# A hand-ordered attention and adapter kernel: one pool of seven PSUM banks, and an order planned by a clock of the engines

## The chip, the core and the metric

The kernel runs on one core of a Trainium2 chip. The core has five engines with queues of their own, each working strictly through its own list: TensorE (PE, with its weight loads shown as PEld), VectorE (DVE), ScalarE (ACT), GpSimd (POOL) and SyncE (SP), which here only issues DMA transfers. PE can write only into PSUM, which has eight banks of 512 float32 per partition; DVE and ACT read the banks and so set them free. The metric is the device time of one execution in microseconds.

## What is computed

One transformer block on 4 sequences of 1024 tokens with 256 channels: layer norm with modulation, attention with 16 heads of 16 channels, then a second layer norm and a mixture of adapters in which each group of tokens takes one of 8 experts by its reconstruction loss. Cut to what matters here:

```python
h = _layernorm(x) * (1 + ca) + sa
qkv = h @ qkv_w.T                                    # per head: q, k, v of 16 channels
scores = einsum('bhqd,bhkd->bhqk', q, k) * scale
probs = softmax(scores, axis=-1)
out = einsum('bhqk,bhkd->bhqd', probs, v)
x = x + ga * (out @ proj_w.T + proj_b)
h = _layernorm(x) * (1 + cb) + sb
base = h @ W_base + b_base
hid = relu(h @ W_enc[n] + b_enc[n])                  # 8 experts
losses = mean((hid @ W_dec[n] + b_dec[n] - h) ** 2)
top1 = argmin(losses)                                # one expert for a group of tokens
mid = relu(h @ W_down[top1] + b_down[top1])
x = x + gb * (base + mid @ W_up[top1] + b_up[top1])
```

## The kernel before, in words

The work of PE falls into three kinds, and the text calls them by these names.

**Scores.** For each of 4 sequences, 4 groups of 4 heads and 2 halves of the queries there is one "hq" (32 in all, in the order of the table `SEQ`). An hq has 32 tiles `M` (queries on the partitions, 512 keys in the free dimension; DVE reduces each to a row maximum, line 1293) and 8 units of 4 tiles `E` (keys on the partitions, 512 queries; ACT takes the exponential of each into `P`, line 1118). That makes 1024 M tiles and 1024 E tiles. Each is one matmul whose contraction is 48 or 50 rows, on the upper or the lower 64 partitions, so that two neighbours of unlike halves run side by side. The maxima of an hq go through `mmax` (DVE, POOL), a short transpose `mturn` (PE), a copy (ACT, `mT`) and four small DMAs into two rows of `QO`, and only then can the E tiles of that hq be computed. The M tiles therefore run ahead of the E tiles, by `LEAD` = 48 tiles here.

**P V.** For each of the 256 units, 4 products of `P` with `V` (17 columns each, side by side) accumulate into the bank `pO`. After 8 units ACT copies it to `osb`, from where it goes through DRAM (`oput`, `oget`, `orec`, `osum`, `onorm`) to the attention output `AT`.

**Side products.** All the rest: `ln1turn` (transposes), `qk` and `v` (projections), `proj`, `xturn`, `enc` (hidden layers of all experts), `gsq` and `half` (the losses), `base`, `select`, `mid`, `out`. Each has an eviction on DVE or ACT. The `qk` results are split into `hi` and `lo` and moved by 12 DMAs per group into `QO` and `KO` (`copy`). The evicting ACT step waits for the copies of the group before, since it overwrites `hi`.

**What sets the order.** `order()` writes one list of steps; every engine goes through the same list and takes from it what is its own. `plan()` names the unit from which a side step may come, and `before()` the steps that it needs, each with a lag in units. The main loop then repeats a fixed cycle: a burst of `BURST` = 3 E tiles and 3 M tiles (M and E in turn), then either one or two units of P V or some side products, whose number follows from a credit (`SHARE`) for each sequence. A side product comes in at most two pieces (`PIECES`).

**Banks.** `pO` has one bank for itself. The other seven are three for M (`MB`), three for E (`EB`) and one for side products (`XB`); a side product also takes a bank of M or E when its own is in use, and score tiles never take the one of the side products. `Steps` writes down which bank a step has. Before a tile PE waits until the reader of the bank's last contents is done (`free0` to `free6`).

The last sequence has a tail written out by hand (`first`, `base`, `now`, `fill`), after the last P V.

## Time and profile before

| | us |
|---|---|
| median of 3 runs | 1006.09 |
| lowest and highest | 1005.58, 1010.55 |
| span of the profiled execution | 1004.2 |
| PE busy | 962.7 (96%) |
| DVE busy | 813.2 (81%) |
| ACT busy | 661.7 (66%) |
| POOL busy | 284.4 (28%) |
| first P V unit to last P V unit | 69.8 to 958.2 |

The profile is read in this way. Busy shares tell which engine is short of time, but a PE that waits inside a burst of pipelined matmuls still looks nearly busy, since the ends of matmuls are modelled. So the starts of matmuls in the timeline are read, from the start of one group of equal work to the start of the next. The waits of PE show in the idle time of its weight loads (PEld) with the instruction that ended it. `x` counts are instructions; a matmul on plain float32 operands (`V` with `P`, `wqkv_s`, `wpg`, `wug`) is recorded as two instructions. `SPq`, `ACTq` are DMA issues on the queues of these engines.

### The profile page before, as it was taken

The numbers are of one execution on the slowest core, as the hardware profiler recorded it, in microseconds if no ns is written. First come the engines' busy times: TensorE is split into PE (matmuls) and PEld (weight loads), VectorE is DVE, ScalarE is ACT, GpSimd is POOL, SyncE is SP. The second block draws the span as 40 slices with busy tenths as digits, with TensorE's granted clock in tenths as the row PEclk, the third lists the DMA queues.
The fourth block names the chain that finished last, engine by engine and source line by source line (L and its number), as shares of the span: only waits on it lengthen the run. The fifth ranks groups of instructions, "written<-read, shape, count | busy, mean of one in ns | idle before, by whom it ended". The sixth has DMA issues, their size and how long they took to land.

```text
span 1004.2 us, 16485 instructions
## 1 busy us (share of the span) xinstructions
PE 962.7 (96%) x5794; PEld 480.8 (48%) x5794; DVE 813.2 (81%) x1657; ACT 661.7 (66%) x1295; POOL 284.4 (28%) x391
## 2 busy tenths in 40 slices
PE   6989999999899999999999999999999999999998
PEld 5444344343344445554454454545454455644476
DVE  4789989899688887788888888788778788889455
ACT  2148787887577777667668786766657767666831
POOL 4210133022155241200336431300237413116320
PEclk9879999999899999999999999999999999999999
DMA  6850051242550513242223511404424311132001
GB/s 180 141 92 23 12 107 45 56 95 71 80 96 12 96 34 66 44 85 81 70 87 60 85 44 45 75 13 78 130 70 80 58 29 35 38 96 77 29 6 48
DMA packets 47890, 66.93 MB, mean 67 GB/s; under 512 B 12139, under 2 KB 32112, under 8 KB 47796
## 3 DMA queue, kind: packets, MB, share of 16 engines
q1 hardware_dynamic: 46572, 65.00, 29.9%
q0 software_dynamic: 384, 0.79, 0.5%
q8 instruction: 46, 0.75, 0.3%
q14 instruction: 36, 0.29, 0.1%
q10 hardware_dynamic: 852, 0.09, 0.1%
HBM read 27.48 MB, written 12.59 MB: 40 GB/s over the span
## 4 chain that ended last, share of the span: by engine, by line
PE 77%; DVE 9%; ACT 5%; issue 2%; POOL 2%; DMA 2%; SPq 1%; ACTq 0%; DVEq 0%; POOLq 0%
PE pE L811 25%; PE pO L811 22%; PE pX L811 18%; PE pM L811 11%; DVE mx L1293 4%; ACT P L1118 2%; DMA QO<-lo 1%; ACT h1T L1159 1%; DVE h2f L1454 1%; ACT h2f L1205 1%; ACT hi L1175 1%; DVE lo L1374 1%; SPq L1867 0%; DVE junk L1430 0%; DMA P<-in_wmod 0%
## 5 line engine op out<-in xcount | busy, mean ns | idle before, releaser
L1293 DVE TENSOR_REDUCE mx<-pM 128x1 f32<-128x512 f32 x1006 | 629.7, 682 | 76.7 <-PE pM L811 71.4
L1118 ACT ACTIVATE P<-pE 128x512 f32<-128x512 f32 x996 | 526.7, 601 | 181.1 <-PE pE L811 177.8
L811 PE MATMUL pM<-KO,QO 48*128 48x512 f32 x1006 | 370.7, 455 | 6.8 <-DMA QO<-lo 3.3
L811 PE MATMUL pE<-QO,KO 50*128 50x512 f32 x996 | 349.2, 438 | 11.9 <-ACT h1T L1159 5.1
L811 PEld LDWEIGHTS pE<-QO,KO 50*128 50x128 f32 x996 | 164.9, 187 | 234.1 <-issue 125.1
L811 PE MATMUL pO<-P,V 128*17 128x512 f32 x2048 | 257.9, 598 | 5.1 <-ACT P L1118 5.1
L811 PEld LDWEIGHTS pM<-KO,QO 48*128 48x128 f32 x1006 | 164.3, 187 | 41.3 <-DVE mx L1293 28.8
L811 PEld LDWEIGHTS pO<-P,V 128*17 128x17 f32 x2048 | 40.5, 96 | 103.2 <-issue 88.1
L1695 POOL CAST mh<-mxc 128x16 fp32r<-128x16 f32 x32 | 6.5, 203 | 285.7 <-DVE mxc L1302 285.5
L811 PE MATMUL pX<-h1T,wqkv_s 128*128 128x512 f32 x112 | 59.2, 642 | 1.9 <-DVE lo L1374 1.5
L1754 POOL TENSOR_TENSOR Hs<-h2f,Hs 128x512 fp32r<-128x512 f32 x28 | 35.7, 1284 | 83.6 <-ACT Hs L1235 68.3
L1374 DVE SCALAR_TENSOR_TENSOR lo<-pX,cst,hi 128x512 fp32r<-128x512 f32 x27 | 20.2, 750 | 28.9 <-ACT hi L1175 28.8
L1175 ACT ACTIVATE hi<-pX,cst 128x512 fp32r<-128x512 f32 x27 | 18.6, 690 | 25.7 <-PE pX L811 20.8
L1721 POOL TENSOR_TENSOR AT<-AT,asum 128x512 f32<-128x512 f32 (+1 forms) x16 | 20.7, 1295 | 48.1 <-DMA asum<-wsum 48.1
L1748 POOL TENSOR_TENSOR Xs<-Xr,Xs 128x512 fp32r<-128x512 f32 x16 | 20.5, 1283 | 38.4 <-ACT Xs L1225 37.4
L811 PEld LDWEIGHTS pX<-h1T,wqkv_s 128*128 128x128 f32 x112 | 18.9, 193 | 23.2 <-issue 19.0
L1792 POOL TENSOR_SCALAR Xr<-x,mv,rs 128x256 f32<-128x256 f32 x24 | 29.3, 1227 | 0.9 <-POOL rs L1780 0.2
L1659 POOL TENSOR_SCALAR xin<-xin,mv,rs 128x256 f32<-128x256 f32 x24 | 29.3, 1228 | 0.5
L811 PE MATMUL pX<-Xs,Hs 128*128 128x258 f32 x192 | 28.6, 294 | 0.2 <-ACT h1T L1159 0.2
L811 PEld LDWEIGHTS pX<-Xs,Hs 128*128 128x128 f32 x192 | 24.4, 189 | 7.6 <-issue 6.2
L1125 ACT ACTIVATE osb<-pO 128x512 f32<-128x512 f32 x32 | 19.3, 602 | 11.1 <-PE pO L811 10.8
L811 PE MATMUL pX<-wqkv_s,h1T 128*128 128x256 f32 x88 | 23.8, 400 | 0.0
(301 smaller groups left out, 1023.4 us busy)
## 6 DMA issues: line engine op xcount, KB each, us to landing
outs<-osb SPq DMA_DIRECT2D x31, 256.0 KB, 2.9
KO<-hi SPq DMA_DIRECT2D x56, 128.0 KB, 4.0
QO<-hi SPq DMA_DIRECT2D x56, 128.0 KB, 5.1
x<-in_x SPq DMA_DIRECT2D x20, 256.0 KB, 3.6
out<-x SPq DMA_DIRECT2D x16, 256.0 KB, 2.1
AT<-outs SPq DMA_DIRECT2D x15, 256.0 KB
asum<-wsum SPq DMA_DIRECT2D x15, 256.0 KB
KO<-lo SPq DMA_DIRECT2D x28, 128.0 KB, 3.6
```

The lines of the kernel that those rows point to most:

```text
L811: return e.matmul(o, lhsT, rhs, start=start, stop=stop)
L1118: e.activation(P[:, u % 3, j, :], bank(s), ACT.Exp).then_inc(*empties(s))
L1125: e.activation(osb[:, :], pO[:, :], ACT.Copy).then_inc(s_osb, 1)
L1159: a = e.activation(h1T[:, c, 256 * k:256 * k + 256], bank(s)[:, 256 * c:256 * c + 256], ACT.Identity, bias=modT[:, c, b:b + 1], scale=modT ...
L1175: e.activation(halves(gi)[0][:, cs], bank(s), ACT.Identity, scale=qscale).then_inc(s_hi, 1)
L1293: e.tensor_reduce(mx[:, hq % 2, k:k + 1, kh], bank(s), AX.X, ALU.max, negate=True).then_inc(*empties(s))
L1374: e.scalar_tensor_tensor(out=lo_[:, cs], in0=bank(s), scalar=qscale, in1=hi_[:, cs].bitcast(F), op0=ALU.mult, op1=ALU.subtract).then_inc(* ...
L1659: a = e.tensor_scalar(xt[:, t, :], xt[:, t, :], mv1[:, k, t, 0:1], rs1[:, k, 1, t:t + 1], ALU.subtract, ALU.mult)
L1721: e.tensor_tensor(rows, rows, asum[0:p1, :], ALU.mult).then_inc(s_at, 1)
L1748: e.tensor_tensor(Xs[:, t0:t0 + 2, 1, 0:D], Xr[:, t0:t0 + 2, :], Xs[:, t0:t0 + 2, 0, 0:D].bitcast(F), ALU.subtract).then_inc(s_Xl, 1)
L1754: e.tensor_tensor(Hs[:, t % 4, :, 1, :], h2f[:, t % 2, :].rearrange("p (a n) -> p a n", a=4), Hs[:, t % 4, :, 0, :].bitcast(F), ALU.subtra ...
L1792: a = e.tensor_scalar(Xr[:, t % 4, :], x2[:, t, :], mv2[:, t, 0:1], rs2[:, 1, t:t + 1], ALU.subtract, ALU.mult)
```

## The change

The seven banks become one tensor `pS` that every kind of step shares. `order()` no longer follows a fixed cycle; it keeps a clock for the two halves of PE (`lane`), for ACT, DVE, POOL and SP (`engine`) and for each bank (`free`), with a table of durations (`WORK`, `GROUP`, `TILE`, `UNIT`, `ENTER`), and asks at each point what comes next:

- in a burst of scores it goes on as long as a bank is free by that clock, and takes M or E by which evicting engine has less work waiting (`BIAS` favours M; M may lead E by up to `AHEAD` = 64 tiles);
- otherwise it takes P V units that are ready, or one *group* of a side product, or goes back to scores. A side product now has up to six groups (`GROUPS`), and scores or P V may stand between them, while its bank stays taken;
- background steps (`quiet`) and copies come by the clock, not by units, and `before()` has no lags.

In `SEQ` the third and fourth group of heads are taken half by half, and in `plan()` the side steps after attention are due in two halves, the first 15 units earlier; `prep` is due at unit 20 for all sequences. Two operands are widened: `wdh`, `wdl` become parts of one tensor, and `mid` runs with 128 columns of weights of which 64 count; `wug` and `mid` have 128 rows, the added ones zero. DVE gets two more memsets at the start and POOL one. The number of score tiles, P V units and side matmuls is the same. The code also has a way to run a side group on one half of the array (`h` not None, `s_over`); the planner never asks for it. The tail written by hand has the same products in the same order.

Cut to its core (comments on steps that are the same are left out):

```diff
-BURST = 3
-SHARE = (1.2, 1.8, 1.8, 2.4)
-LIGHT = 66
-MB, EB, XB = (0, 1, 2), (3, 4, 5), 6
+BANKS = 7
+GROUPS = {"qk": 2, "v": 4, "proj": 4, "enc": 6, "half": 4, "gsq": 4, "base": 4, "mid": 6, "out": 6,
+          "ln1turn": 1, "xturn": 1}
-SEQ = [(gi, c) for gi in range(4 * NB - 3) for c in range(2)]
-SEQ += [(4 * NB - 3 + g, c) for c in range(2) for g in range(3)]
+SEQ = [(4 * b + g, c) for b in range(NB - 1) for g, c in (
+    (0, 0), (0, 1), (1, 0), (1, 1), (2, 0), (3, 0), (2, 1), (3, 1))]
+SEQ += [(4 * NB - 4 + g, c) for g, c in (
+    (0, 0), (0, 1), (1, 0), (2, 0), (3, 0), (1, 1), (2, 1), (3, 1))]
+TILE, UNIT, AHEAD = 228, 853, 64
+SOON, PATIENCE = 200, 2000
+BIAS, ONE, FED, TICK = 300, 900, 500, 700
+LATE, NEED = 0, 5
+LIGHTLY, HEAVY = (500, 500, 500, 0), (4000, 4000, 3000, 2000)
+ENTER = {"S": 260, "V": 110, "X": 110}
...
-            halves = ((B - 23, (0, 1)), (B, (2, 3))) if q == LAST else ((B, (0, 1, 2, 3)),)
+            halves = ((B - (23 if q == LAST else 15), (0, 1)), (B, (2, 3)))
...
-            u = B + (20 if b == LAST else 53)
+            u = B + 20
...
     if kind == "qk":
-        return [(("ln1turn", b, 2 * a[1] + i), 1) for i in range(2)] + [(("moved", 4 * b + a[0] - 1), 2)]
+        return [("ln1turn", b, 2 * a[1] + i) for i in range(2)] + [("moved", 4 * b + a[0] - 1)] + (
+            [("v", b, k) for k in range(4)] if a == (3, 1) else [])
...
+    def score(r):
+        t = flow.lane[r]
+        if flow.bank(t + LATE) is None:
+            return None
...
+        return min(found, key=lambda f: flow.backlog(f[0]) - BIAS * (f[0] == "DVE"))[1]
...
+    while min(e) < 2 * NU:
+        background()
+        t = flow.now()
+        found = [score(0), score(1)]
+        s = found[0] or found[1]
+        if mode == "S" and s:
+            if all(found) and sorted(flow.free)[1] <= max(flow.lane) + LATE:
+                flow.lane = [max(flow.lane)] * 2
+                r = 0 if found[0][0] == "M" else 1
+                take(found[r], r)
+                take(score(1 - r) or found[1 - r], 1 - r)
+                continue
+            if not all(found):
+                take(s, found.index(s))
+                continue
+        n = weighable()
+        busy = min(flow.backlog("ACT"), flow.backlog("DVE"))
...
+        if mode != "S" and p > (HEAVY if busy < FED else LIGHTLY)[min(pv // UB, LAST)] and side():
+            continue
+        if mode != "S" and s and (busy < FED or vacant(t + ENTER["S"] + 300) >= NEED):
+            enter("S")
+            continue
+        if n >= 2 or n and (min(e) >= 2 * (pv + 3) or mode == "V" or busy > ONE):
+            weigh(min(n, 2))
+            continue
+        if (p > LIGHTLY[min(pv // UB, LAST)] or not s) and side():
+            continue
...
-        pM = ctx.enter_context(nc.psum_tensor("pM", [128, 3, 512], F))
-        pE = ctx.enter_context(nc.psum_tensor("pE", [128, 3, 512], F))
+        pS = ctx.enter_context(nc.psum_tensor("pS", [128, BANKS, 512], F))
         pO = ctx.enter_context(nc.psum_tensor("pO", [128, 512], F))
-        pX = ctx.enter_context(nc.psum_tensor("pX", [128, 512], F))
...
+            if kind == "mid":
+                c, i = divmod(g, 3)
+                sl = slice(512 * s[2], 512 * s[2] + 512)
+                wh, wl = (wdhl[r, k:k + 2, :].rearrange("p a n -> p (a n)") for k in (c, 2 + c))
+                return thrice(o, wh, wl, h2h[r, c, sl], h2l[r, c, sl])[i:i + 1]
```

What this makes of PE's list, counted over the whole of it (a group is a row of equal kind; the transposes `mturn` count as side products):

| | scores: groups | P V: groups | side: groups | matmuls |
|---|---|---|---|---|
| before | 342 (314 of 6 tiles, 22 of 4, 5 of 12, 1 of 16) | 189 (67 of two units) | 192 | 2048, 1024, 1407 |
| after | 405 (48 of 2 tiles, 163 of 4, 148 of 6, 34 of 8, 12 longer) | 239 (17 of two units) | 247 | 2048, 1024, 1407 |

Of these, 81, 63 and 26 groups stood between the first and the 64th P V unit, and now 87, 61 and 37; from there to the 240th unit 232, 116 and 142, and now 289, 165 and 187.

The first place is PE early in the first sequence, where there is hardly any side work. `free3` and the like are the banks that a tile waits for. Before:

```order
L811 MATMUL pE<-QO,KO 128x512 [waits free5]
L811 MATMUL pM<-KO,QO 128x512 [waits free0]
L811 MATMUL pE<-QO,KO 128x512 [waits free3]
L811 MATMUL pM<-KO,QO 128x512 [waits free1]
L811 MATMUL pE<-QO,KO 128x512 [waits free4]
L811 MATMUL pM<-KO,QO 128x512 [waits free2]
L811 MATMUL pO<-P,V 17x512 x4
```

and now:

```order
L1072 MATMUL pS<-KO,QO 128x512 [waits free3]
L1072 MATMUL pS<-QO,KO 128x512 [waits free0]
L1072 MATMUL pS<-KO,QO 128x512 [waits free2]
L1072 MATMUL pS<-QO,KO 128x512 [waits free5]
L1072 MATMUL pS<-KO,QO 128x512 [waits free4]
L1072 MATMUL pS<-QO,KO 128x512 [waits free1]
L1072 MATMUL pS<-QO,KO 128x512 [waits free6]
L1072 MATMUL pS<-KO,QO 128x512 [waits free0]
L1072 MATMUL pO<-P,V 17x512 x4
```

The burst went from six tiles on banks tied to their kind to eight tiles on any bank; the eighth takes the bank of the second.

The second place is PE at the side work of the third sequence (beside the scores of the fourth), at its last transposes and at loss products. `cst,Xr` are the transposes `xturn`, `Hs` are products of `gsq`, `Xs,Hs` of `half`. Before:

```order
L971 MATMUL pX<-cst,Xr 128x128 [waits X,free6]
L971 MATMUL pX<-cst,Xr 128x128 x3
L971 MATMUL pE<-cst,Xr 128x128 [waits free3]
L971 MATMUL pE<-cst,Xr 128x128 x3
L811 MATMUL pE<-QO,KO 128x512 [waits free4]
L811 MATMUL pM<-KO,QO 128x512 [waits free0]
L811 MATMUL pE<-QO,KO 128x512 [waits free5]
L811 MATMUL pM<-KO,QO 128x512 [waits free1]
L811 MATMUL pE<-QO,KO 128x512 [waits free3]
L811 MATMUL pM<-KO,QO 128x512 [waits free2]
L811 MATMUL pX<-Hs 128x256 [waits Hl,free6]
```

and now, at the same transposes:

```order
L1243 MATMUL pS<-cst,Xr 128x128 [waits X,free2]
L1243 MATMUL pS<-cst,Xr 128x128 x3
L1072 MATMUL pS<-KO,QO 128x512 [waits free4]
L1072 MATMUL pS<-KO,QO 128x512 [waits free5]
L1072 MATMUL pS<-QO,KO 128x512 [waits d_m13,free1]
L1072 MATMUL pS<-QO,KO 128x512 [waits d_m10,free3]
L1072 MATMUL pS<-KO,QO 128x512 [waits free0]
L1072 MATMUL pS<-QO,KO 128x512 [waits free6]
L1072 MATMUL pO<-P,V 17x512 x4
L1243 MATMUL pS<-cst,Xr 128x128 [waits free2]
L1243 MATMUL pS<-cst,Xr 128x128 x3
L1072 MATMUL pS<-KO,QO 128x512 [waits free4]
```

The second transpose, which took the bank of an E tile (`free3`) just ahead of a burst whose last pair wanted it back, now stands behind that burst and a P V unit and takes the bank of the first transpose.

The third place is PE at the `enc` products of the same side work. Where one `enc` (six matmuls) stood in one piece, it is now cut by score groups:

```order
L1072 MATMUL pO<-P,V 17x512 x4
L1072 MATMUL pS<-weh,h2h 128x512
L1072 MATMUL pS<-KO,QO 128x512 [waits free4]
L1072 MATMUL pS<-QO,KO 128x512 [waits d_m02,free3]
L1072 MATMUL pS<-KO,QO 128x512 [waits free2]
L1072 MATMUL pS<-QO,KO 128x512 [waits free0]
L1072 MATMUL pS<-KO,QO 128x512 [waits free1]
L1072 MATMUL pS<-QO,KO 128x512 [waits free5]
L1072 MATMUL pS<-wel,h2h 128x512
L1072 MATMUL pS<-weh,h2l 128x512
L1072 MATMUL pS<-weh,h2h 128x512 [waits free3]
L1072 MATMUL pS<-QO,KO 128x512 [waits free4]
```

One matmul of an `enc` stands alone between a P V unit and a burst, and the product keeps its bank over the burst.

## Rows read from the trace of the kernel before

**Rows 1.** The page: busy time of the engines, and TensorE's clock in 40 slices.
```profile
PE 962.7 (96%) x5794; PEld 480.8 (48%) x5794; DVE 813.2 (81%) x1657; ACT 661.7 (66%) x1295; POOL 284.4 (28%) x391
...
PEclk9879999999899999999999999999999999999999
```

**Rows 2.** Busy time by stretch: us, PE, PEld, DVE, ACT, POOL (x), PEclk, DMA share, GB/s.
```profile
69.80:257.20 187.40, 184.37 (x1108) 75.53 (x1110) 169.79 (x298) 148.49 (x289) 38.48 (x61) 0.99 0.29 63
257.20:918.50 661.30, 642.05 (x3967) 320.53 (x3966) 544.10 (x1103) 455.09 (x896) 198.67 (x256) 0.99 0.30 65
...
958.20:1004.20 46.00, 40.80 (x277) 35.72 (x276) 29.32 (x103) 9.24 (x18) 7.03 (x9) 1.00 0.08 27
```

**Rows 3.** Timeline of PE, 793 to 806 us: start, length, instruction, count, idle before.
```profile
793.05 1.91 PE L811 MATMUL pO<-P,V 128*17 128x512 f32 x16
794.89 0.50 PE L811 MATMUL pE<-QO,KO 50*128 50x512 f32 x1
...
795.23 0.63 PE L811 MATMUL pE<-QO,KO 50*128 50x512 f32 x2
...
795.80 0.50 PE L811 MATMUL pX<-weh,h2h 128*128 128x512 f32 x1
...
797.52 0.39 PE L811 MATMUL pE<-wel,h2h 128*128 128x512 f32 x1
797.75 0.40 PE L811 MATMUL pE<-weh,h2l 128*128 128x512 f32 x1
798.08 0.50 PE L811 MATMUL pE<-QO,KO 50*128 50x512 f32 x1
...
799.42 1.05 PE L811 MATMUL pO<-P,V 128*17 128x512 f32 x8
800.41 0.50 PE L811 MATMUL pE<-QO,KO 50*128 50x512 f32 x1
...
803.35 0.49 PE L811 MATMUL pE<-QO,KO 50*128 50x512 f32 x1
...
805.08 0.50 PE L811 MATMUL pE<-QO,KO 50*128 50x512 f32 x1 [0.99 <-ACT h2f L1205]
...
805.51 0.74 PE L811 MATMUL pX<-Hs 128*128 128x256 f32 x4
```

**Rows 4.** Timeline of PE: the first and the last groups of scores and of P V.
```profile
26.84 1.19 PE L811 MATMUL pM<-KO,QO 48*128 48x512 f32 x3 [3.33 <-DMA QO<-lo]
...
69.77 1.91 PE L811 MATMUL pO<-P,V 128*17 128x512 f32 x8
...
954.44 0.50 PE L811 MATMUL pM<-QO,KO 50*128 50x512 f32 x1
...
955.11 1.05 PE L811 MATMUL pO<-P,V 128*17 128x512 f32 x8
957.15 1.05 PE L811 MATMUL pO<-P,V 128*17 128x512 f32 x8 [0.99 <-ACT P L1118]
```

**Rows 5.** Waits, whole span: us in total, times, longest us.
```profile
PEld pE L811 <- ACT P L1118: 60.4, 88, 0.9
PEld pM L811 <- DVE mx L1293: 29.7, 92, 2.2
```

**Rows 6.** The page: costliest groups of the two evicting engines.
```profile
L1293 DVE TENSOR_REDUCE mx<-pM 128x1 f32<-128x512 f32 x1006 | 629.7, 682 | 76.7 <-PE pM L811 71.4
L1118 ACT ACTIVATE P<-pE 128x512 f32<-128x512 f32 x996 | 526.7, 601 | 181.1 <-PE pE L811 177.8
```

**Rows 7.** Timeline, 264 to 267 us, and the clock's stretch behind it.
```profile
264.85 0.69 ACT L1175 ACTIVATE hi<-pX,cst 128x512 fp32r<-128x512 f32 x1 [4.60 <-DMA QO<-lo]
...
266.07 1.05 PE L811 MATMUL pO<-P,V 128*17 128x512 f32 x8 [3.17 <-ACT P L1118]
...
268.00:274.00 6.00, 6.00 (x13) 2.35 (x12) 2.66 (x6) 2.54 (x6) 0.58 (x3) 0.50 0.08 30
```

**Rows 8.** Groups by shape: a matmul of `mid`, on 64 columns of weights.
```profile
L811 PE MATMUL pX<-h2h,wdl 128*64 128x512 f32 x12 | 4.7, 394 | 0.0
```

More of the change, by code:

```diff
@@ new lines, in order @@
+    late |= {("out", q, i) for i in range(4)} | {("xsq", q, 1)} | set(sums(q, 0)) | set(sums(q, 1))
+    rest = [s for k in ("quiet", "short", "long") for s in waiting[k] if s not in late]
+    while rest:
+        s = min(rest, key=lambda s: max([done.get(p, 1e18) for p in before(s)] + [flow.now()]))
+        rest.remove(s)
+        if s[0] in BANKED:
+            flow.alone(s, sum(GROUP.get(s[0], 300) for g in range(groups(s))) if s[0] in GROUPS else 300)
+            out[-1:] = whole(s)
+            del flow.banks[s]
+        else:
+            flow.quiet(s)
@@ L1019, in tensor @@
+                    if part.over:
+                        a.then_inc(s_over, 1)
+                    elif part.last:
                         a.then_inc(*fills(s))
@@ L1468, in vector @@
                     dve.wait_ge(*emptied(*s))
-                elif kind == "gsq":
+                elif kind == "gsq" and last:
                     b, i, th = s[1:]
```

915 lines of the change are left out of this document (511 added, 404 removed).

## Prediction

> **What bounds the kernel now.** I read the page first. PE is busy for 96% of the span, DVE for 81%, ACT for 66%, and the clock was at its upper level nearly throughout [rows 1]. So PE is the engine to look at, with DVE behind it. The busy time by stretch says where: up to the 64th P V unit DVE is busy for 169.8 of 187.4 us (91%), from there to the 240th unit for 544.1 of 661.3 us (82%), ACT for 79% and 69% [rows 2].
>
> A PE at 96% can still be waiting, so next comes the timeline of PE, read from the start of one group of equal work to the start of the next. A clean burst of six score tiles takes 0.91 us, from 794.89 to 795.80, and two P V units take 1.84 us, from 793.05 to 794.89; one unit takes 0.99 us, from 799.42 to 800.41 [rows 3]. The next clean thing to read is the pitch inside a group. The second pair of tiles starts 0.34 us after the first [rows 3], and further pairs follow at 0.23 us, as do matmuls of the same 512 columns (797.52 to 797.75). The last matmul of a group is followed by a start of another kind only after 0.33 us (797.75 to 798.08) [rows 3]. So one change of kind costs some 0.1 us. In sum I price a group of scores at 0.228 us a pair plus 0.205 us (0.89 for six tiles), P V at 0.858 a unit plus 0.125 us, and each further group of side work at 0.095 us.
>
> Bursts are often not clean. The one at 803.35 needs 2.16 us until 805.51; its last pair waits for a bank that ACT holds with `h2f`, a side product that had borrowed a bank of E [rows 3]. Between the first and the last group of scores [rows 4] there are 342 groups. Start to next start they take 397.6 us in all; at the price above they would take 342 x 0.205 + 1024 x 0.228 = 303.6 us. So PE **waits 94.0 us inside score groups**: 9.5 before the first P V unit, 24.0 up to the 64th, 56.8 up to the 240th, 3.7 after. P V groups add 6.6 us (189 groups from 69.77 to 957.15 take 249.9 us, priced 243.3); 955.11 to 957.15 is one with a wait [rows 4]. By cause, the weight loads of E tiles idle 60.4 us for ACT and those of M tiles 29.7 us for DVE [rows 5]. Yet in the same run DVE idles 71.4 us for an M tile, and ACT 177.8 us for an E tile [rows 6]. PE waits for banks of one kind while the engine of the other kind has nothing to do.
>
> **The change, part by part.** The sum is made against the profiled execution, 1004.2 us; the median of the runs is 1.9 us above it.
>
> *More groups.* By the counts of the order, scores go from 342 to 405 groups, P V from 189 to 239, side work from 192 to 247. That is 63 x 0.205 = 12.9, 50 x 0.125 = 6.3 and 55 x 0.095 = 5.2, together **+24.4 us** on PE, certain, since the order is fixed. 48 of the new score groups are of one pair; none is in the trace. Between the pitch of a pair (0.23) and the first step of a burst plus the change of kind (0.34 + 0.1) I take the price formula, 0.43; the lower end would take 48 x 0.2 = 10 us off. The bursts are *shorter* than before (5.1 tiles on average for 6.0), whatever the rule about free banks.
>
> *The waits of today.* All 94.0 + 6.6 - 9.5 = 91 us from the first P V unit on are open to the change, because every one of them hangs on the order or on whose bank it is. So are 3.4 us in which the clock stood at 0.50 after a stall (268 to 274 and a little around it) [rows 7]. Together **-94.5 us**. What lies before the first P V unit and behind the last (46.0 us [rows 2]) keeps its order and its products, and I cost it at nothing.
>
> *The waits of tomorrow, W.* The span is then 1004.2 + 24.4 - 94.5 + W = 934.1 + W. This is the one unknown term, and I bound it. From below: up to the 64th unit PE would need 187.4 - 24.4 + 2.0 = 165 us, DVE has 169.8 us of work [rows 2], so W is at least 5. From above: as many waits as today, 91 us, or more, if DVE becomes what PE waits for. From the 64th to the 240th unit PE's clean time becomes 661.3 - 56.8 - 5 - 3.4 + 22 = 618 us, and DVE's 544 us [rows 2] are then 88% of it. The nearest stretch with such a share is the first one, at 91%, where 24.0 of 187.4 us were waits (13%); at today's 82% it was 8.6%. But those shares belong to banks fixed at three, three and one. With seven interchangeable banks, M allowed to lead by 64 tiles rather than 48, and the side products cut into groups between which scores can pass, the idle 71.4 us of DVE [rows 6] and the wait at 803.35 are just what should shrink. I take half of today's waits: 14 us in the first stretch (DVE at 95% there), 31 us for the rest, **W = 45**. At the second place of the order the `xturn` pair that caused the wait at 803.35 is indeed parted by a burst and a P V unit.
>
> *Edits with one answer.* The wider `mid` keeps its 512 columns, and on 64 columns of weights these take 394 ns, on 128 columns 0.40 us [rows 3, 8]; the wider `wug` streams the same 256 columns. The extra memsets run before DVE's first data has come, at most 1 us if that cover is gone. The copies and the quiet steps keep their number; only their places move. An `enc` that stays open over a burst holds one of the seven banks for some 2 us longer, which is part of W.
>
> One rule speaks against the change. The Trainium skill, *TensorEngine Tiling (Array Packing)*, Key Properties, says that changing the tiling mode drains TensorE. Scores (64 rows), P V (32 columns) and side work (whole array) are three modes, and the order now changes kind 891 times where it changed 723 times. The rows show the same as the 0.1 us between kinds [rows 3]; the page alone would say that the time gets longer. The term of +24.4 us above comes from rows alone.
>
> **The rivals.**
>
> *Near the floor.* The clock of the planner matches the pitches that the trace shows (228 against 0.23 us, 853 against 0.858), so its order might fit nearly everywhere: W = 17, which gives 951 us. Against it: landings of DMAs and side evictions vary, and every engine is strictly in order.
>
> *Waits as before.* The banks are what is short, not their assignment: each shorter burst is followed by the same wait elsewhere, W = 70, and the time is 1006 us. For it speaks that the planned bursts got shorter, which says that banks are rarely free.
>
> *DVE takes over, slower.* Place: the side work from the 64th to the 240th unit. If PE waits there for DVE at the first stretch's rate, 13% of 618 us = 80 us, and 24 us in the first stretch as now, W = 104, the span 1038 and the time 1040 us; half way to it, W = 87, gives 1023. It decides above W = 70: there the removed waits no longer pay for the 168 new changes of kind. For it: DVE alone has 629.7 us of M reductions [rows 6] which no order shortens. In the Trainium skill, the same page under Performance Considerations says that a faster TensorE may find PSUM evacuation the bottleneck and advises to use both ScalarE and VectorE for it; here every M tile goes to DVE. By that rule it would be this rival.
>
> *Long stalls by landings.* The lags of two units before a `qk` are gone; its step comes when the copies should have landed by the clock. At 264.85 ACT had stood 4.60 us for such a copy, PE stood 3.17 us at the P V behind it, and the clock then fell to 0.50 [rows 7], about 6.6 us in all. ACT is in order, so all exponentials are queued behind the waiting step. Six such stalls, W = 45 + 40, give 1021 us; from four on the gain is under the bound. The same holds for the four small DMAs of a maximum, with a lead down to 40 tiles where it was 48.
>
> **How the numbers follow.** Forecast 934.1 + 45 + 1.9 = 981 us: chance 0.50, its own range W 25 to 63, 961 to 999. Near the floor 0.12 (951). Waits as before 0.14 (1006). DVE takes over 0.16 (1023 to 1040). Landings 0.08 (1021). The range leaves out half of the two outer cases' tails: 952 to 1021. What can be told from no change for this kernel is about 0.5%, 5 us. Faster by more: 0.50 + 0.12, and a little from the third case, 0.64. Within 0.5%: 0.13. Slower: 0.23.
>
> **What the changed profile would show.** Right: score groups of four tiles at 0.66 us clean, waits inside them of some 40 us in total, DVE's idle time for M tiles well under 71.4 us, DVE at 83% of the span, PE's waits for ACT's `P` down to a third. The added groups: start-to-start sums of P V at 0.983 us for nearly all 239. Wrong: waits of PE for DVE above 60 us (DVE takes over), gaps above 2 us in PE's timeline with a clock at 0.50 behind them (landings), or the first stretch, up to the 64th unit, above 187 us although it has hardly any side work.

## The result

| | median us | runs | span of the profiled execution |
|---|---|---|---|
| before | 1005.86 | 1005.58 to 1010.55 | 1004.2 |
| after | 1016.93 | 1013.59 to 1020.07 | 1013.5 |

(More runs of the kernel before stand behind this median than ahead of the prediction.) The changed kernel is slower: after / before is 1.0095, with an interval of 1.0068 to 1.0122. I had forecast 981 us, faster. The time lies in the stated range of 952 to 1021 us, but it moved the other way.

The page of the changed kernel, busy time and TensorE's clock, for [rows 1]:

```profile
PE 980.8 (97%) x5794; PEld 464.4 (46%) x5794; DVE 814.4 (80%) x1659; ACT 663.6 (65%) x1295; POOL 284.3 (28%) x392
...
PEclk9878999999999999999989999999999999979999
```

Busy time by stretch, for [rows 2]: from the first P V unit to the 64th, from there to the 240th, the last 16 units, and what follows the last P V. Then three short stretches with a low clock. Columns as there.

```profile
69.24:271.24 202.00, 197.35 (x1136) 74.95 (x1138) 172.60 (x307) 152.00 (x296) 48.03 (x72) 0.96 0.30 64
271.24:928.76 657.52, 650.92 (x3954) 308.08 (x3952) 546.74 (x1105) 454.90 (x890) 196.96 (x256) 0.99 0.29 64
928.76:967.38 38.62, 36.52 (x228) 13.53 (x226) 17.28 (x36) 31.52 (x65) 10.76 (x12) 1.00 0.11 37
967.38:1013.50 46.12, 40.91 (x276) 36.43 (x276) 29.38 (x103) 9.21 (x18) 6.04 (x8) 1.00 0.08 27
64.40:81.50 17.10, 16.96 (x66) 8.07 (x66) 11.30 (x21) 9.32 (x18) 0.00 (x0) 0.50 0.67 93
511.60:518.40 6.80, 6.80 (x27) 1.80 (x26) 4.67 (x9) 3.80 (x8) 1.27 (x1) 0.50 0.03 9
897.30:907.50 10.20, 10.10 (x34) 5.29 (x32) 8.77 (x17) 4.31 (x9) 2.35 (x4) 0.50 0.35 101
```

The first stretch is 14.6 us longer (202.0 for 187.4), the second 3.8 us shorter (657.5 for 661.3), the third 1.1 us shorter (38.6 for 39.7); the rest is as it was within 0.6 us. The page's groups of the evicting engines, for [rows 6], and PE's waits, for [rows 5]:

```profile
L1500 DVE TENSOR_REDUCE mx<-pS 128x1 f32<-128x512 f32 x1024 | 643.0, 682 | 91.0 <-PE pS L1072 84.7
L1323 ACT ACTIVATE P<-pS 128x512 f32<-128x512 f32 x1024 | 542.1, 603 | 213.4 <-PE pS L1072 210.7
```

```profile
PEld pS L1072 <- ACT P L1323: 47.0, 94, 0.9
...
PEld pO L1072 <- ACT P L1323: 23.9, 52, 1.8
PEld pS L1072 <- DVE mx L1500: 23.7, 51, 2.3
```

PE waits less for banks than before: 47.0 and 23.7 us at the weight loads of score tiles, 60.4 and 29.7 before. (The loads of P V idle more for ACT, 23.9 us for 13.0, but PE's own starts show little of it, as the account says.) DVE idles 84.7 us for M tiles, 71.4 before, and ACT 210.7 us for 181.3 (177.8, and 3.5 for the 28 E tiles that stood in banks of M): in the longer run both wait more for PE.

**The account.** I set each group of PE (start to next start) against the price of the prediction, with 0.2 us instead of 0.095 for a side group, and split what is left over by whether the clock stood at 0.50 somewhere in the group. The matmuls of the side products are priced at 228.6 us in all four. From the first P V unit to the end of the last:

| us | before | after | e1 | e12 |
|---|---|---|---|---|
| length | 888.4 | 898.1 | 873.2 | 861.6 |
| groups of scores, P V, side | 329, 189, 178 | 392, 239, 233 | as before | 355, 235, 150 |
| priced work | 800.9 | 831.8 | 800.9 | 806.9 |
| waits at full clock | 82.5 | 42.3 | 63.6 | 53.0 |
| over the price where the clock was 0.50 | 5.0 | 24.0 | 8.7 | 1.8 |
| time at 0.50 | 10.0 | 32.7 | 13.7 | 3.6 |

So +9.7 us is +30.9 of groups, -40.2 of waits and +19.0 in stretches at half clock. (Against e1 it is +24.9: +30.9, -21.3 and +15.3.) "Over the price" at half clock holds both the slower matmuls and any waits in those groups.

Two more things stand in the same starts. First, where the score groups wait. In the trace of before, groups of up to six tiles were 76.8 us over their price and longer ones 7.8; in e1 it is 62.9 and 5.6; in the changed kernel 22.9 and **40.0**, the latter in 45 groups of eight tiles or more. A burst of eight is never clean: the fastest of the 34 takes 1.64 us, and the price is 1.12. The planner knows of this wait: by its clock such a burst takes 1.42 us at the least. Against e1 the short bursts lose 40.0 us over the price and the long ones add 34.4. No run caps them at six, so what that would bring is not shown; the fastest order, e12, has 48 such groups with 31.2 us.

Second, the longest stretch at half clock is the one in which P V begins, 64.4 to 81.5; 12.3 of its 17.1 us lie behind the first P V unit, and the groups there are 6.0 us over their price. In the trace of before this drop ended at 72.9, and the groups at half clock in the first stretch were 1.5 us over their price. So a good part of the 14.6 us of the first stretch is here; 18 side matmuls that now come before the 65th unit are another part.

The next longest begins at 897.3. PE's timeline ahead of it (start, length, instruction, count, idle before):

```profile
893.00 0.27 PE L1126 MATMUL pS<-cst,mhl 128*32 128x128 f32 x1
893.23 1.10 PE L1072 MATMUL pS<-KO,QO 48*128 48x512 f32 x2
895.02 1.10 PE L1072 MATMUL pS<-KO,QO 48*128 48x512 f32 x2 [0.70 <-DVE mx L1500]
896.82 3.78 PE L1072 MATMUL pS<-KO,QO 48*128 48x512 f32 x8 [0.70 <-DVE mx L1500]
900.40 1.99 PE L1072 MATMUL pS<-QO,KO 50*128 50x512 f32 x4
902.20 0.62 PE L1072 MATMUL pS<-KO,QO 48*128 48x512 f32 x1
...
904.07 1.91 PE L1072 MATMUL pO<-P,V 128*17 128x512 f32 x8
```

The `mturn` of an hq comes only at 893.00. Until its DMAs land no E tile can be computed, and the plan fills the gap with 15 M tiles of a row of 22 score tiles. DVE takes them one by one and PE goes at its pace: it is busy for 2.48 of the 4.07 us from 893.23 to 897.30. From 897.3 on the clock is at its lower level (1.2 GHz). The row takes 8.1 us more than its price.

### The profile page after: what moved, and what is told of

It reads as the page before. It is cut to its first block, busy times and chain, and to the rows that moved or that the text cites. A ratio compares the mean times of both kernels' runs of the same rounds, so it can differ in the third digit from the quotient of the medians.

```text
span 1013.5 us, 16489 instructions
## 1 busy us (share of the span) xinstructions
PE 980.8 (97%) x5794; PEld 464.4 (46%) x5794; DVE 814.4 (80%) x1659; ACT 663.6 (65%) x1295; POOL 284.3 (28%) x392
## 4 chain that ended last, share of the span: by engine, by line
PE 83%; DVE 7%; ACT 4%; DMA 2%; issue 1%; POOL 1%; SPq 1%; ACTq 0%; DVEq 0%; POOLq 0%
PE pS L1072 57%; PE pO L1072 23%; DVE mx L1500 4%; ACT P L1323 3%; PE pS L1243 1%; DMA xin<-in_x 1%; PE pS L1126 1%; DMA QO<-lo 1%; DVE lo L1581 1%; DMA P<-in_wmod 0%; SPq L2075 0%; ACT hi L1380 0%; DVE h2f L1661 0%; SPq L2061 0%; ACT h2f L1410 0%
## 5 line engine op out<-in xcount | busy, mean ns | idle before, releaser
L1500 DVE TENSOR_REDUCE mx<-pS 128x1 f32<-128x512 f32 x1024 | 643.0, 682 | 91.0 <-PE pS L1072 84.7
L1323 ACT ACTIVATE P<-pS 128x512 f32<-128x512 f32 x1024 | 542.1, 603 | 213.4 <-PE pS L1072 210.7
L1072 PE MATMUL pS<-KO,QO 48*128 48x512 f32 x1024 | 354.7, 454 | 9.9 <-DMA QO<-lo 4.3
L1072 PE MATMUL pS<-QO,KO 50*128 50x512 f32 x1024 | 345.3, 450 | 2.7 <-DVE mx L1500 0.6
L1072 PEld LDWEIGHTS pS<-KO,QO 48*128 48x128 f32 x1024 | 161.0, 190 | 233.9 <-issue 178.5
L1072 PEld LDWEIGHTS pS<-QO,KO 50*128 50x128 f32 x1024 | 157.8, 189 | 69.2 <-issue 42.5
L1072 PEld LDWEIGHTS pO<-P,V 128*17 128x17 f32 x2048 | 35.1, 95 | 88.4 <-issue 60.4
L1072 PE MATMUL pS<-h1T,wqkv_s 128*128 128x512 f32 x128 | 68.8, 649 | 2.0 <-ACT h1T L1364 1.2
L1072 PE MATMUL pS<-Xs,Hs 128*128 128x258 f32 x384 | 55.7, 292 | 0.4 <-DVE mx L1500 0.3
L1072 PEld LDWEIGHTS pS<-Xs,Hs 128*128 128x128 f32 x384 | 48.9, 190 | 9.5 <-issue 7.6
L1380 ACT ACTIVATE hi<-pS,cst 128x512 fp32r<-128x512 f32 x30 | 20.6, 688 | 30.1 <-PE pS L1072 30.0
L1072 PE MATMUL pS<-wpg,AT 128*128 128x256 f32 x128 | 36.7, 402 | 0.1
L1661 DVE TENSOR_TENSOR h2f<-pS,nbe 128x512 f32<-128x512 f32 x32 | 21.8, 683 | 13.6 <-PE pS L1072 13.4
```

The lines of the kernel that those rows point to most:

```text
L1072: return e.matmul(o, lhsT, rhs, start=start, stop=stop)
L1323: e.activation(P[:, u % 3, j, :], bank(s), ACT.Exp).then_inc(*empties(s))
L1380: e.activation(halves(gi)[0][:, cs], bank(s), ACT.Identity, scale=qscale).then_inc(s_hi, 1)
L1500: e.tensor_reduce(mx[:, hq % 2, k:k + 1, kh], bank(s), AX.X, ALU.max, negate=True).then_inc(*empties(s))
L1661: e.tensor_tensor(h2f[:, t % 2, :], bank(s), nbe[:, :], ALU.max).then_inc(*empties(s))
```

## The experiments

All runs are compared with runs of the kernel before on the same chip (medians 1006.5 to 1009.0). One more quantity is used from e9 on: what the *planner* takes by its own clock, from `lane` at the start of the first P V unit to `lane` at the end of the last. It is called the plan below. Where two kernels are compared by their traces, each trace is one execution.

**e1: pooled banks under the old order.** The kernel before; each score tile and each side product takes the bank that was used longest ago and that no open side product holds (the score tiles' lines).

```diff
-                bank = min(EB, key=lambda x: at.get(x, -1))
+                bank = self.pooled(unfinished, at)
...
-                bank = s[1] % 5 if s[1] < LEAD else min(MB, key=lambda x: at.get(x, -1))
+                bank = s[1] % 5 if s[1] < LEAD else self.pooled(unfinished, at)
```

> The order of the kernel before, step for step; only the banks differ: every score tile and side product takes the one of seven banks that was used longest ago. Theory A (today's 94 us of waits inside score groups hang on whose bank a tile may take): the waits fall by a third to a half, the time to 965 to 980 us. Theory B (the fixed cycle of 3 and 3 tiles is what makes PE wait, the assignment is second to it): 1000 to 1008 us.

Measured: 990.64 us, ratio 0.982 (0.978 to 0.986), between the two expectations. The pool is worth 15 to 17 us by itself, and no group is added. This run is faster than both kernels, so it is the new order that loses, some 26 us. (The changed kernel also has the widened operands, which e1 has not; e12 has them too and is faster than e1.)

**e2: side products in one piece.** The changed kernel, with this at the head of the main loop:

```diff
+        if opened:
+            side()
+            continue
```

> The changed kernel, but a side product that is begun is finished before anything else comes: 142 side groups for 247, 323 score groups for 405. Theory C (the changes of kind eat the gain, 0.2 us for each group of side work or of scores): 187 groups less give -38 us, against some more waits, so 980 to 990 us. Theory D (stretches in which PE has only scores and runs at the pace of DVE and ACT, and the half clock behind them, eat the gain): such stretches remain (four bursts of 14 tiles), 1000 to 1015 us.

Measured: 1017.27 us, 1.009 (1.006 to 1.012), no other than the changed kernel and above both expectations. The account says why that is no proof of no effect: priced work fell by 38.1 us (793.7), and waits at full clock rose from 42.3 to 89.3. The starts say where: the score groups of eight tiles or more went from 45 to 103, and they are 73.9 us over their price where they had been 40.0.

**e3: maxima turned at once.**

```diff
-SOON, PATIENCE = 200, 2000
+SOON, PATIENCE = 200, 0
```

> The changed kernel with PATIENCE 0 for 2000: the transpose of the maxima goes in as soon as the clock of the planner has them, so that no E tiles are held up and the bursts of 22 and 14 tiles at 893 and 508 us are gone (longest in the main part: 12). The number of groups falls by 21 only, worth 4 us. Theory D: the two stretches and the half clock behind them cost 17 to 20 us, so 995 to 1003 us. Theory C: 1010 to 1014 us.

Measured: 1019.04 us, 1.010 (1.007 to 1.013), above both expectations. Half-clock time between the P V units is 35.8 us, at other places than in the changed kernel (346.9, 364, 589.3 and 947.7 us in place of 511.6 and 897.3). The drop in which P V begins is there as in the changed kernel (to 80.7). The two long rows of the changed kernel are not *the* cause.

**e4: old SEQ and due units.** The changed kernel, with `SEQ`, the due units after attention and those of `prep` from the kernel before.

> The changed kernel with the order of heads (SEQ) and the due units of the kernel before: side work after attention in one piece, later. Theory D: whether a long burst stands somewhere decides; here none above 10 tiles after the first, so 1000 to 1008 us. If the halves and early dates were what pays, it is slower than the changed kernel: 1020 us or more. Theory C: 1015 to 1018 us, since the groups are as many (409, 235, 243).

Measured: 1009.23 us, 1.002 (0.999 to 1.004), some 8 us less than the changed kernel and just above the expectation of theory D.

Its ten executions show how much one kernel moves: from 1004.73 us at a mean granted clock of 0.986 to 1015.66 us at 0.971, some 7 us for each 0.01, an estimate from these two. The four of the changed kernel stand at 0.969 to 0.976, those of the kernel before that have a clock on record at 0.981 to 0.990. Waits and a low clock come together, and this does not say which brings the other.

**e5: the new SEQ and due units under the old order**, with the pool (e1).

> The kernel before with the seven banks pooled (e1), and with the changed kernel's SEQ and its due units as well; the fixed cycle of bursts stays. Undoing SEQ and due units in the changed kernel took 8 us off. If these dates put the side work in a worse place under any order, this run is 5 to 12 us slower than e1: 996 to 1003 us, and the stretch behind the 64th unit is dearer. If they only hurt together with the planner's order, it is within 3 us of e1: 988 to 993 us.

Measured: 989.64 us, 0.983 (0.980 to 0.986), as the second expectation had it. The dates cost nothing under the fixed order; under the planner they do.

**e6: the new order on banks of three kinds.** The changed kernel's list of steps, only the bank is chosen by kind. The rule is stricter than that of the kernel before: there a second side product in a row goes to a bank of M or E, here it waits for the one bank of its kind unless that product is still open.

```diff
-            if s in chosen:
-                bank = chosen[s]
+            if s in chosen and s[0] in ("E", "M"):
+                mine = range(5) if s[0] == "E" and m == 1024 else (0, 1, 2) if s[0] == "M" else (3, 4, 5)
+                bank = min((i for i in mine if i not in over), key=lambda x: at.get(x, -1))
+                m += s[0] == "M"
+            elif s in chosen:
+                bank = 6 if 6 not in over else min((i for i in range(6) if i not in over), key=lambda x: at.get(x, -1))
```

> The changed kernel's order, step for step, but the banks go by kind again: three for M, three for E, one for side products (another one only while that is taken). It shows what the new order is worth without the pool. If the pool only gave the planned order what the fixed order got from it too (15 us), the time is 1028 to 1036 us. If the order leans on the pool, since bursts of eight tiles, rows of M alone and an open side product need banks of any kind, the time is 1045 to 1090 us, with the waits of PE inside score groups back above 80 us. If the kind of a bank does not matter to this order, 1012 to 1020 us.

Measured: 1284.55 us, 1.273 (1.268 to 1.279), far above every expectation. PE, then DVE:

```profile
476.44 2.07 PE L1077 MATMUL pS<-h1T,wqkv_s 128*128 128x512 f32 x2
480.07 3.78 PE L1077 MATMUL pS<-wqkv_s,h1T 128*128 128x256 f32 x8 [1.56 <-DVE lo L1586]
```

```profile
479.27 0.75 DVE L1586 SCALAR_TENSOR_TENSOR lo<-pS,cst,hi 128x512 fp32r<-128x512 f32 x1 [1.81 <-ACT hi L1385]
```

A `v` product behind a `qk` product waits on the one bank for side work until `hi` and `lo` are written. Such places and the clock go together: 274 of the 1172 us between the P V units are at half level, and the side groups take 470.5 us there where the changed kernel's take 271.6. The 268 us are what this rule costs the new order, the greater part of them in side work; what the rule of the kernel before would cost it is not shown, and so 268 can't be set against the 15 of e1. That the new order leans on the pool is shown.

**e7: e4 with M preferred more.**

```diff
-BIAS, ONE, FED, TICK = 300, 900, 500, 700
+BIAS, ONE, FED, TICK = 900, 900, 500, 700
```

> The changed kernel with the old SEQ and due units (as e4, 1009 us) and BIAS 900 for 300: M is taken earlier, so that its lead over E never falls to 40 tiles, and the planned long rows of scores without P V (22 and 14 tiles) go; the longest row now has 14 tiles. If a wait inside such a row, and the clock at half level behind it, is what the changed order loses, the half-clock stretches between the first and the last P V unit fall from 29 to under 16 us and the time to 996 to 1001 us. If the drops come wherever PE waits some 2 us, they move to other places, and the time stays at 1005 to 1012 us.

Measured: 1007.25 us, 1.001 (0.998 to 1.003), the second expectation. The time at half clock did fall, from 29.0 to 10.3 us, and the excess there from 16.6 to 6.9. But waits at full clock rose by 5.7, and from the first to the last P V unit it gained only 2.6, no more than executions of one kernel differ by. `BIAS` changes the order too, so this is not the clock alone taken away. What it does show: at a median granted clock of 0.988, where e1 has 0.986, this order still takes 16.6 us more than e1. So the clock is not what keeps the new order behind e1. Against the kernel before it may be: with as high a clock e7 is level with it, and the 19.0 us of the account are more than the whole +9.7.

**e8: the price of a group.** e1 with 197 bursts parted by one whole-array product, whose result the next tile overwrites.

```diff
+                if n in parting:
+                    pe.wait_ge(s_wen, 2)
+                    mm(o[:, 0:64], weh[:, 0, 0:128], weh[:, 0, 0:64])
```

> The pooled kernel with the fixed order (e1), in which 197 of the bursts of six score tiles between the 88th and the 240th unit are parted: ahead of the third pair PE does one whole-array matmul of 64 columns, whose result the next tile overwrites. It measures the price of a further side group and a further score group. By the prediction's price (0.095 + 0.205 us, and 0.03 for the 64 columns) a parted burst without a wait takes 0.91 + 0.33 = 1.24 us from its start to the next group, by the price that the changed kernel's trace shows for a side group (0.2) 1.34 us. The 197 are 65 or 85 us of PE time; what the run is longer than e1 (990.6 us) by is this less what the waits inside bursts give back. If such waits give back hardly anything the time is 1055 to 1076 us; if they give back half, 1025 to 1040 us.

PE's timeline of one parted burst:

```profile
701.20 0.49 PE L814 MATMUL pE<-QO,KO 50*128 50x512 f32 x1
...
701.53 0.40 PE L814 MATMUL pM<-QO,KO 50*128 50x512 f32 x1
701.86 0.30 PE L814 MATMUL pE<-weh 128*128 128x64 f32 x1
702.09 0.50 PE L814 MATMUL pE<-QO,KO 50*128 50x512 f32 x1
...
702.52 1.91 PE L814 MATMUL pO<-P,V 128*17 128x512 f32 x16
```

It takes 1.32 us, 701.20 to 702.52, where a clean burst takes 0.91 [rows 3]: 0.41 for one more score group and one more side group, of which some 0.03 is the product itself (an estimate, 0.23 x 64/512). It is no odd case: more than 150 of the 197 take 1.31 to 1.33 us. I had priced the two at 0.205 + 0.095. The run took 1046.41 us, 55.8 more than e1, of the 81 us (197 x 0.41) that were added: the waits inside bursts gave back a third, between the two expectations. A wait takes the place of a group's price only in part.

**e9: a dearer table.** e4, with durations nearer to those of the rows: an M reduction is 643.0/1024 = 0.63 us busy, an exponential 542.1/1024 = 0.53.

```diff
-TILE, UNIT, AHEAD = 228, 853, 64
+TILE, UNIT, AHEAD = 228, 858, 64
...
-        name, ns = ("ACT", 478) if s[0] == "E" else ("DVE", 600)
+        name, ns = ("ACT", 495) if s[0] == "E" else ("DVE", 620)
...
-ENTER = {"S": 260, "V": 110, "X": 110}
+ENTER = {"S": 300, "V": 125, "X": 150}
```

> The changed kernel with the old SEQ and due units (e4), and dearer durations in the planner's table, nearer to the pitches in the traces: 620 ns for 600 for an M tile on DVE, 495 for 478 for an E tile on ACT, 300, 125 and 150 ns for entering scores, P V and side work where it had 260, 110 and 110. By its own clock the planner takes 860.7 us from the first to the last P V unit in e4, and the chip took 886.1 (25.4 more); with the dearer table the same rules plan 884.1 us. If the cheap table is what the plan is wrong by, the chip takes 884 to 892 us there, and the whole kernel 1005 to 1013 us: a truer clock, and no better order. If the difference comes from what no table holds (the clock at half level, landings), it stays 20 to 30 us: 904 to 914 us, 1024 to 1036 us in all. If a plan on a truer clock makes fewer waits, it is under 1000 us.

Measured: 1014.96 us, 1.006 (1.004 to 1.008), just above the first expectation. Between the P V units the chip took 882.7 us for 884.1 planned. As 18.7 us of them were at half clock, which no plan holds, part of this agreement is errors that cancel. Behind them it took 62.6 us instead of 46: side work was left over, which I had not expected.

**e10: knobs searched on that clock.** BIAS 600, ONE 600, FED 1300, LATE 150, SOON 350, AHEAD 60, and other thresholds for side work (`LIGHTLY`, `HEAVY`).

> The kernel e9 (dearer table, old SEQ and due units) with other knobs of the planner: BIAS 600, ONE 600, FED 1300, LATE 150 (PE may wait 0.15 us for a bank before it closes a burst), SOON 350, AHEAD 60, and other thresholds for side work. By its own clock it plans 835.9 us from the first to the last P V unit, the shortest of some two thousand settings. If the planner's clock can be trusted to some 10 us, the chip takes 840 to 855 us there and 962 to 977 us in all, less than the fixed order with pooled banks (990.6). If the shortest plan is one that errs most in its own favour, the chip takes 870 to 890 us there, and 990 to 1010 us in all.

Measured: 1038.39 us, 1.030 (1.028 to 1.033), far above both expectations. The two stretches, up to the last P V unit and behind it:

```profile
71.65:907.66 836.01, 827.24 (x4995) 367.05 (x4994) 696.61 (x1328) 620.44 (x1221) 218.67 (x301) 1.00 0.29 62
907.66:1034.37 126.71, 93.44 (x581) 81.48 (x580) 68.30 (x217) 20.71 (x41) 43.15 (x46) 0.91 0.13 40
```

836.0 us for 835.9 planned: the planner's clock held here. But the search had found the plan that puts 80 us of side work behind the last P V, where nothing runs beside it. What is optimised must hold the tail.

**e11: M leads by 56 tiles, in e1** (`LEAD = 56`).

> The pooled kernel with the fixed order (e1, 990.6 us), and M leads by 56 tiles rather than 48. The changed kernel lets M lead by up to 64, and its lead falls to 40 at one place, where PE waits 8 us. If the lead is what E tiles wait for under the fixed order too, 982 to 988 us; if 48 tiles are enough there, 988 to 993 us.

Measured: 1005.31 us, 0.998 (0.996 to 0.999), worse than both expectations. Eight more M tiles stand ahead of the first P V (74.1 us for 69.4), and the clock is at half level for 10.2 us from 790.4 and for 6.9 from 892.8. I did not trace the rest.

**e12: the true clock, the tail counted, side products whole.** e9 and the edit of e2, with knobs by the plan including side work left behind: BIAS 450, FED 1300, SOON 500, `HEAVY` 8000 for the first three sequences.

> The kernel e9 (dearer table, old SEQ and due units) with side products in one piece, as in e2, and knobs chosen by the planner's own clock, this time with the side work counted that is left behind the last P V unit (e10's plan had pushed it there): BIAS 450, FED 1300, SOON 500 and side work taken earlier only above 8000. It plans 864.2 us from the first to the last P V unit and leaves nothing behind it but the tail written by hand. In e9 and e10 the dearer table met the chip to 1.4 and 0.1 us (882.7 for 884.1 planned, 836.0 for 835.9). If the plan is good to 5 us again, 69.5 + 864 + 46 + 2 = 982 us, 976 to 988 us, less than the fixed order with pooled banks (990.6). If the planner's order loses on something that its clock does not hold, 995 to 1015 us.

Measured: **978.91 us**, 0.9705 (0.9689 to 0.9721), the fastest of all and within the first expectation, 861.6 us for 864.2 planned.

```profile
PEclk9879999999999999999999999999999999999999
```

```profile
69.48:931.12 861.64, 844.82 (x5306) 395.38 (x5304) 732.06 (x1444) 628.39 (x1249) 254.61 (x339) 1.00 0.29 65
931.12:977.24 46.12, 40.88 (x277) 36.40 (x276) 29.32 (x103) 9.22 (x18) 5.95 (x8) 1.00 0.08 27
```

```profile
L1502 DVE TENSOR_REDUCE mx<-pS 128x1 f32<-128x512 f32 x1024 | 636.8, 681 | 40.1 <-PE pS L1074 35.5
```

DVE idles 35.5 us for M tiles (84.7 in the changed kernel), and from 73.1 us to the end the clock does not drop.

**e13 to e15: one difference put back into e12 each.** e13: the cheap table. e14: side products cut (the three lines of e2 out). e15: the new `SEQ` and due units.

> e12 (978.9 us) with nothing changed but the planner's table, back at the changed kernel's cheap values (600, 478, entering 260, 110, 110). By its own cheap clock it plans 848.3 us between the P V units, 16 less than e12. If the cheap table is what sends plan and chip apart, the chip takes 868 to 878 us there (in the changed kernel and e2 it took 28.6 and 35.1 more than planned) and 986 to 996 us in all. If the table is not what matters, but the knobs and whole side products are, the chip takes 858 to 866 us there and 976 to 983 us in all.

> e12 with side products cut by scores and P V again, as in the changed kernel; table and knobs stay. The clock plans 874.6 us between the P V units and leaves 43 us of side work behind them; there are 84 more groups of scores and 106 more of side work. If the plan holds, 69.5 + 917 + 44 = 1031 us, 1022 to 1040 us. If cutting costs no more than it brings, as e2 against the changed kernel said under the cheap table, 977 to 990 us.

> e12 with the changed kernel's SEQ and due units; with this the whole difference to the changed kernel is the table, four knobs and whole side products. The clock plans 866.0 us, nothing left behind. If the dates matter only by way of what the planner makes of them, 979 to 987 us. If they cost by themselves, as the 8 us between the changed kernel and e4 would have it, 986 to 992 us.

Measured: e13 990.57 us, 0.983 (0.980 to 0.987), +11.7 on e12, as the text expected of a cheap table. e14 1047.44 us, 1.038 (1.035 to 1.041), +68.5, above the 1031 that the plan gave (and its range up to 1040), with 52.7 us at half clock. Most of this is not the cutting as such: in the two traces, 76.4 us apart, 28.5 lie between the P V units and 47.9 behind the last, where this plan left side work over (94.1 us for 46.1). It is e10's trap again. e15 992.46 us, 0.986 (0.983 to 0.989), +13.6, just above the expectation that dates cost by themselves. But e5 says that they don't. The plan for e15 is only 1.8 us longer than that for e12, and why the chip adds 6.5 us to it stays open.

**Plan and chip**, us from the first to the last P V unit:

| | table | plan | chip | chip - plan | at half clock |
|---|---|---|---|---|---|
| after | cheap | 869.5 | 898.1 | 28.6 | 32.7 |
| e2, side whole | cheap | 866.8 | 901.9 | 35.1 | 32.1 |
| e3, turned at once | cheap | 870.0 | 900.1 | 30.1 | 35.8 |
| e4, old dates | cheap | 860.7 | 886.1 | 25.4 | 29.0 |
| e7, BIAS 900 | cheap | 866.1 | 883.5 | 17.4 | 10.3 |
| e13 | cheap | 848.3 | 872.8 | 24.5 | 19.1 |
| e9 | dearer | 884.1 | 882.7 | -1.4 | 18.7 |
| e10 | dearer | 835.9 | 836.0 | 0.1 | 4.3 |
| e12 | dearer | 864.2 | 861.6 | -2.6 | 3.6 |
| e15, new dates | dearer | 866.0 | 872.5 | 6.5 | 9.7 |
| e14, side cut | dearer | 874.6 | 890.1 | 15.5 | 52.7 |

With the cheap table the chip is 17 to 35 us behind the plan, with the dearer one within 7 except for e14. The chip's column is the traced execution; that of e14 took 8.0 us more than the median of its four, that of e15 2.9 less. Up to the 64th P V unit the changed kernel's plan has 185.1 us and the chip took 202.0, so 16.9 of the 28.6 us arise in the first stretch. Six numbers were made dearer together; which of them it is I did not separate. The prices of entering a kind are the least likely: in the changed kernel's plan they add up to some 154 us for the 392, 239 and 233 groups, and by the prices of the account these groups cost 156.9 (both are estimates). So most of the 28.6 us must be waits that the plan has not, the 24.0 us over the price at half clock among them.

## Why the prediction was wrong

*What bounds the kernel* held in part: PE waited for banks of one kind, and pooling them gave 15 us (e1). But under the fixed order the score groups were still 68.5 us over their price, 84.6 before, so most of today's waits did not hang on the kind of the bank.

*More groups, +24.4 us, "certain".* It came to +30.9. The term for side work, 0.095 a group, was mis-sized: I had taken the change of kind once, but the first step of the next group is also longer, and e8 has 0.38 for a side and a score group together where I had 0.30. The new groups of one pair take 0.43 us at the median, as priced. (The other 0.7 us are three more pairs of score tiles that now stand behind the first P V unit.) The Trainium skill, *TensorEngine Tiling (Array Packing)*, Key Properties, says that a change of tiling mode drains TensorE; the rows agree with it, at the 0.38 us of e8.

*The waits of tomorrow, W = 45, is the step that failed.* It was to hold everything over the price, and that came to some 70 us. Plain waits at full clock inside score and P V groups did come out at 46.4 us (45.1 and 1.3), but this meets my 45 by luck: I had taken half of today's waits, and 40.0 us of what the score groups wait is in long bursts that I had not looked at. Another 24.0 us over the price stand in stretches at half clock, 19 more than before. By place, W was some 29 us in the first stretch where I had 14, and 42 behind it where I had 31. I had removed today's 3.4 us of clock and allowed none for tomorrow, although [rows 7] showed the clock at 0.50 behind one stall of 3.17 us. Taken together W is 70.4, the value of the rival *waits as before*; with it and 6.5 us more for groups the span is 934.1 + 70.4 + 6.5 = 1011.0, of the 1013.5 measured. So the step failed by 25 us in the term that decided the sign. Side groups, which run 1.4 us less under their price than before, make most of the rest.

Behind it is a step that I left out: I never asked what the plan itself takes. I wrote that "the clock of the planner matches the pitches that the trace shows" from two of its numbers (228 and 853) and did not look at the 600 for an M tile, though [rows 6] say 629.7 us busy for 1006 of them. The plan is 869.5 us between the P V units, against 888.4 in the trace of before: at its own word 19 us less, not 25, and 3.7 less than what e1 gets from the pool alone. Then the chip adds 28.6.

*The edits with one answer* held: up to the first P V unit 69.2 us for 69.8, behind the last 46.1 for 46.0; a matmul of the widened `mid` takes 395 ns in e12, 392 before (`h2l` with its weights). That the halved dates and the new `SEQ` were not costed at all was a gap of 8 to 14 us under the planner's order (e4, e15).

*The rivals.* "DVE takes over" named the right side and the wrong mechanism: its sign was waits of PE for DVE above 60 us, and they fell from 29.7 to 23.7 us while DVE idled more. The Trainium skill, same page, Performance Considerations, warns that PSUM evacuation may become the bottleneck; the trace does not bear that out for the kernel as a whole, only for rows such as the one at 893. *Waits as before* had the right total, W = 70, and "the same wait elsewhere" is what the bursts of eight show; it missed the clock and the 6.5 us of groups. "Long stalls by landings" has one case, the 8.1 us at 893; e3 and e7 show that removing such places alone brings nearly nothing. "Near the floor" is excluded (its 951 us was a span; as a time, with the 1.9 us that the others have, it is 953). That 1016.93 lies in the stated range is no success: my own case ended at 999, and only the rivals reached further.

*What the changed profile would show.* Right: a clean group of four tiles takes 0.66 us, P V's waits at full clock are nearly gone (1.3 us). Half right: waits inside score groups, said to be some 40 us, are 45.1 at full clock, but 62.9 with the groups at half clock. Wrong: PE's waits for ACT's `P`, said to fall to a third, fell from 60.4 to 47.0 us. DVE's idle time, said to be well under 71.4 us, was 84.7; its share, said to be 83%, was 80%. The sign that I had named for failure, the first stretch above 187 us with hardly any side work, is there: 202.0 us, with DVE busy for 85% of it where it had been 91%. In this stretch DVE is the scarcest engine behind PE, and under the new order it idles for 29.4 us of it, 17.6 before.

**What the loss is made of**, by experiment: from e12 to the changed kernel are 38 us. Put back into e12 one at a time, the cheap table costs 12 us, the dates 14, the cut side products 68, of which most lies behind the last P V unit; they do not add up, since each changes the plan that the others act on, and under the changed kernel's knobs cut or whole makes no difference (e2). That the order loses 26 us against e1, and that the same planner wins 12 against it once its durations are dearer, its dates the old ones, its side products whole, three knobs and `HEAVY` moved and the tail counted, is shown. That one of these *is* the cause is not.

## What to carry to other kernels

When an order comes from a planner with a clock, read off the plan's own length first and set it against the trace of before: it is about the most that the order can bring (no plan here was beaten by more than 2.6 us), and each duration in its table must be checked against a row before it is believed. Price a new group by a run or a row in which a group is really added, and expect waits to absorb only a part of that price (a third in e8). Look at waits by the length of the burst: here the short bursts lost theirs and the long ones took them on. Split a change into pool and order before judging either: here one was worth 15 us and the other cost 26.

## What the runs showed of the hardware

- One whole-array product of 64 columns between two pairs of row-tiled score matmuls lengthened a burst by 0.41 us (e8, 701.20 to 702.52 against 0.91 us).
- In a row of only M tiles PE went at the pace of DVE and was busy for 2.48 of 4.07 us (893.23 to 897.30), with no idle time above 0.70 us; behind that the clock stood at 0.50 for 10.2 us, in which PE counts as busy for 10.10. In e12 the clock stands at 1.00 from 73.2 to 977.2 us.
- One kernel's executions differ with the clock: ten of e4 go from 1004.73 us at a mean granted clock of 0.986 to 1015.66 at 0.971.
- Seven banks split by kind into three, three and one, with side products kept to the one, made the same list of matmuls 26% slower than seven pooled ones (1284.55 for 1016.93 us).
